# A four-stage transformer block on one core: group statistics, masks and the first output chunk placed elsewhere in the retention stage

## The reference

```
qkv = (x @ wqkv.T).reshape(b, s, N_HEADS, 3 * HEAD_DIM).transpose(0, 2, 1, 3)
q, k, v = jnp.split(qkv, 3, axis=-1)
q, k = _xpos_rotary(q, k, s)
scores = jnp.einsum('bhid,bhjd->bhij', q, k) * decay        # decay is 0 above the diagonal
ret = jnp.einsum('bhij,bhjd->bhid', scores, v)
mean = ret.mean(axis=(2, 3), keepdims=True)                 # one mean and variance for each head
var = ret.var(axis=(2, 3), keepdims=True)
ret = (ret - mean) / jnp.sqrt(var + EPS)
ret = ret * gn_weight[None, :, None, None] + gn_bias[None, :, None, None]
y = ret.transpose(0, 2, 1, 3).reshape(b, s, HIDDEN)
g = x @ wg.T
mish = g * jnp.tanh(jax.nn.softplus(g))
return mish * y @ wo.T
```

## Time and profile before

| | |
|---|---|
| median of 3 runs | 1471.06 us (1469.83 to 1471.92) |
| profiled execution | 1483.77 us |
| its span, first to last instruction | 1482.0 us |
| mean granted TensorE clock | 0.877 |
| busy: PE, DVE, ACT, POOL | 1206.4 (81%), 817.6 (55%), 520.3 (35%), 551.0 (37%) us |
| retention in the trace | about 648 to 838 us |
| scans: first, second | 696 to 744 us, 763 to 794 us |

### The profile page before, as it was taken

How to read it: one execution, slowest core, us unless ns; L and a number is a source line. 1 busy time by engine, 2 the same in 40 slices (tenths; PEclk the granted TensorE clock), 3 DMA queues, 4 the chain that set the end, 5 groups by cost and what they waited for, 6 DMA issues and landing times. The chain is left out here.

```text
span 1482.0 us, 19589 instructions
## 1 busy us (share of the span) xinstructions
PE 1206.4 (81%) x6248; PEld 702.8 (47%) x6287; DVE 817.6 (55%) x1572; ACT 520.3 (35%) x1052; POOL 551.0 (37%) x564
## 2 busy tenths in 40 slices
PE   5589999999999599989998515699999998879541
PEld 2242222222222356755565511188889887754220
DVE  6499999999995564433344379712222211115554
ACT  1137777777778231202342100023333332220000
POOL 6003357655356300021200105444444443224665
PEclk9799999999999799999986755589999999888755
DMA  4950531344000400000000100189999999952333
GB/s 133 182 142 12 87 52 28 39 55 53 12 12 12 164 0 1 1 1 1 0 1 1 59 0 1 50 252 307 309 314 315 297 293 230 231 170 64 85 114 99
DMA packets 142583, 154.78 MB, mean 104 GB/s; under 512 B 50673, under 2 KB 111442, under 8 KB 142418
## 3 DMA queue, kind: packets, MB, share of 16 engines
q1 hardware_dynamic: 106882, 98.71, 26.5%
q0 software_dynamic: 12288, 33.57, 9.0%
q10 hardware_dynamic: 23312, 21.24, 4.4%
HBM read 118.34 MB, written 32.51 MB: 102 GB/s over the span
## 5 line engine op out<-in xcount | busy, mean ns | idle before, releaser
L495 ACT ACTIVATE l_ret_store<-attn_st 128x512 f32<-128x512 f32 x512 | 280.0, 599 | 104.1 <-PE attn_st L406 87.8
L519 DVE TENSOR_REDUCE attn_neg<-attn_mx 128x8 f32<-128x1024 f32 x256 | 299.1, 1201 | 13.5 <-PE attn_mx L386 12.6
L1705 DVE COPY exp_y_sb<-exp_y_ps 128x256 f32<-128x256 f32 x160 | 68.0, 425 | 293.0 <-PE exp_y_ps L1650 277.5
L1616 POOL DMA_INDIRECT exp_rows<-x_rows,moe_tok_i x160 | 151.4, 946 | 193.5 <-PE exp_xt_ps L1630 173.9
L1641 PE MATMUL exp_h_ps<-exp_xt,exp_w 128*88 128x128 f32 x1280 | 174.6, 281 | 20.1 <-DMA exp_w<-in_w 19.2
L1650 PE MATMUL exp_y_ps<-exp_w,exp_ht 96*128 96x256 f32 x640 | 171.1, 391 | 3.0 <-ACT exp_ht L1677 3.0
L386 PE MATMUL attn_mx<-attn_k_st,attn_q_st 96*128 96x512 bf16 x512 | 154.9, 384 | 17.7 <-DVE attn_neg L519 15.0
L406 PE MATMUL attn_st<-attn_q_st,attn_k_st 128*128 128x512 bf16 x473 | 160.1, 383 | 5.8 <-DMA attn_q_st<-attn_neg_rows 2.7
L1641 PEld LDWEIGHTS exp_h_ps<-exp_xt,exp_w 128*88 128x88 f32 x1280 | 150.9, 161 | 29.2 <-DMA exp_w<-in_w 27.1
L418 PE MATMUL attn_o<-l_ret_store,l_ret_tab 128*32 128x512 f32 x1024 | 136.4, 605 | 2.8 <-ACT l_ret_store L495 0.8
L1670 ACT ACTIVATE exp_xt<-exp_xt_ps 128x256 f32<-128x256 f32 x160 | 61.3, 383 | 212.8 <-PE exp_xt_ps L1630 206.7
(11 more groups left out here) (233 smaller groups left out, 1666.4 us busy)
## 6 DMA issues: line engine op xcount, KB each, us to landing
exp_w<-in_w SPq DMA_DIRECT2D x320, 176.0 KB
y_rows<-exp_y_sb ACTq DMA_DIRECT2D x160, 128.0 KB
parts<-l0b_front SPq DMA_DIRECT2D x32, 192.0 KB
attn_k_st<-parts SPq DMA_DIRECT2D x48, 128.0 KB, 7.4
attn_q_st<-parts SPq DMA_DIRECT2D x48, 128.0 KB, 8.0
l_ret_tab<-in_tables SPq DMA_DIRECT2D x4, 1024.0 KB
exp_rows<-x_rows,moe_tok_i POOLq DMA_INDIRECT x160
keep_x_t<-in_x_t SPq DMA_DIRECT2D x4, 512.0 KB
```

The source lines that it names most:

```text
L495: act.activation(probs[s % 2][:, h], st_ps[n % BANKS][:], ACT.Exp, scale=SCALE0).then_inc(exp_done, 1)
L519: dve.tensor_reduce(neg[m % 2][:, i], mx_ps[slot["score", n] % 2][:].rearrange("p (j k) -> p j k", k=P), AX.X, ALU.max, negate=True).then_ ...
L1616: pool.indirect_dma_start(rows[b % RB][:], None, a["x_rows"], bass.IndirectOffsetOnAxis(ap=tok_i[:, b:b + 1], axis=0)).then_inc(rows_in[b ...
L1705: dve.tensor_copy(y_sb[b % YB][:], y_ps[b % 2][:, 0:E]).then_inc(y_in, 1)
```

## The change

Four moves, all in retention; nothing is computed otherwise.

- PE, batch 1: `group(0)` is issued ahead of the four gates of batch 1 instead of behind them.
- DVE, both batches: `mask(first)` comes ahead of the lowering of the gates; the two `lower` follow the first and the second mask.
- PE: `out(0)` to `out(3)` are issued inside the second scan, each behind `retain` of the steps 4 to 7 of it, with the wait for all gates behind the first step.
- DVE: the adds of tiles 0 to 3 go into and right behind the second scan's masks, followed by `norm_measure(0)`, all ahead of `moments(1)`; behind the second coefficients comes `norm_scale(0)` and only then `add(1)`.

```diff
--- before.py
+++ after.py
@@ -1140,10 +1140,11 @@
                     turn_k(t)
                 pe.wait_ge(consts, 6)
                 states(b)
+                if b:
+                    group(b - 1)
                 for n in range(b * QC * KT, (b + 1) * QC * KT):
                     gate(n)
                 if b:
-                    group(b - 1)
                     pe.wait_ge(gvar, b)
                 pe.wait_ge(rot_done, HALF_ROT * (b + 1))
                 scores(first)
@@ -1153,9 +1154,10 @@
                     if b == 0:
                         project(HALF_ROT + t)
                     retain(t)
-            pe.wait_ge(g_done, len(gates))
-            for t in range(TC):
-                out(t)
+                    if b and t == first:
+                        pe.wait_ge(g_done, len(gates))
+                    if b and t - first >= KTS - TC:
+                        out(t - first - (KTS - TC))
             group(BATCH - 1)
             for t in range(TC, 2 * TC):
                 out(t)
@@ -1306,10 +1308,13 @@
                 at = ret[:, m, c * CH:(c + 1) * CH]
                 dve.tensor_tensor(at, at, mish[:, m, c * CH:(c + 1) * CH], ALU.mult).then_inc(weighed, 1)
 
+            def add_tile(t):
+                dve.wait_ge(made, t + 1)
+                norm_add(dve, norm, t, a_ps[t % 2][:, 0:E])
+
             def add(c):
                 for t in range(c * TC, (c + 1) * TC):
-                    dve.wait_ge(made, t + 1)
-                    norm_add(dve, norm, t, a_ps[t % 2][:, 0:E])
+                    add_tile(t)
 
             dve.wait_ge(loaded, 16 * (len(RET_W) + 6))
             for n in range(HALF_ROT):
@@ -1319,22 +1324,25 @@
                 sum_states(b)
                 if b:
                     coefficients(b - 1)
-                for c in range(b * QC, (b + 1) * QC):
-                    lower(c)
                 for t in range(b * KTS, (b + 1) * KTS):
                     mask(t)
+                    if t % KTS < QC:
+                        lower(b * QC + t % KTS)
                     if b == 0:
                         rotate(HALF_ROT + t)
                     elif t % 2:
                         weigh(t % KTS // 2)
+                    if b and t % KTS > KTS - TC:
+                        add_tile(t % KTS - (KTS - TC) - 1)
+                if b:
+                    add_tile(TC - 1)
+                    norm_measure(dve, norm, 0)
                 moments(b)
                 for c in range(b * QC, (b + 1) * QC):
                     close_mish(c)
-            add(0)
             coefficients(BATCH - 1)
-            norm_measure(dve, norm, 0)
+            norm_scale(dve, norm, 0)
             add(1)
-            norm_scale(dve, norm, 0)
             for n in range(QC * KT, 2 * QC * KT):
                 weigh(n)
             norm_measure(dve, norm, 1)
```

## The result

The changed kernel takes 1455.92 us, median of 6 runs (1452.86 to 1460.18), against 1470.73 us for the kernel before in 6 runs of the same comparison (1465.13 to 1476.65). The ratio is 0.9898 with a 95% interval of 0.9879 to 0.9917: some 15 us less (12 to 18). The profiled execution took 1456.11 us, its span 1454.4 us, its mean granted clock 0.890 (0.877 before). All ratios in this text are of executions in the fast state; two slow ones, 2411.94 us among the four of e4 and 1498.36 us among the eight of e6, are left out of them.

The account below looks back on a forecast made before the run. PE was taken to bound the second scan, at half clock. Scan end 782.7 plus 20.0 behind it minus 0.7 gives 802.0 against 815.06, 13.1 us less, so 1458.0 us; the forecast's own range was 1454.5 to 1461.

Parts of the forecast that it names:

- First scan, 0.7 us: First scan of retention: the first mask, now ahead of the lowerings, starts 0.7 us earlier, and all of it is kept.
- Entry: Entry of second scan: scores at 762.0 instead of 762.71, mask 762.8 instead of 765.16, PE's holes 0.8 and 0.15 us.
- Does the clock hold?: Entry of second scan: the granted clock was taken to hold at full level; the lower bound was "falls as before".
- The scan: Second scan at full clock: from 765.05, seven retains 10.4 us and six scores 4.3; end 782.7 with the outputs.
- Outputs inside: Second scan: three output blocks before the last retain, 0.98 us each, put 2.95 us onto PE's path.
- Behind the scan: From the scan's end to the last weighing: 20.0 us, 1.0 less than before, with add(1) taken at 4.8.
- Chunks 1 to 3: Work after the last weighing: order unchanged, clock dips may move, one pair of outs 1.8 us either way.
- rival 1: The clock falls at the second scan's entry and the outs raise it: 3.6 us less, 1467.5 us, chance 0.12.
- Rivals 2 and 3: Clock falls and stays low: in the scan, 1472.7 us, chance 0.07; also through the tail, 1474.8 us, chance 0.06.
- Rival 4: Runs without profile keep full clock in the old second scan: 1 us less, 1470 us, chance 0.10.

Follow-up runs that it names:

- e4: The changed kernel with the first output chunk back behind the second scan (group and mask edits kept); ratio to the kernel before 0.9869.
- e6: The kernel before with the group edit alone (group matmul ahead of the gates); ratio to the kernel before 0.9924.
- e11: e6 plus one full-array matmul of unused result on PE between the first two scores of the second scan; ratio to the kernel before 0.9898.
- e2: The changed kernel with the group matmul back behind the gates (mask and output edits kept); ratio to the kernel before 0.9919.
- e3: The changed kernel with both lowerings back ahead of the masks (group and output edits kept); ratio to the kernel before 0.9878.
- e7: The kernel before with the mask edit alone (first masks ahead of the lowerings); ratio to the kernel before 0.9889.
- e10: e6 unchanged, profiled once more on another chip; one execution, 1462.42 us.
- e8: The changed kernel with POOL's root of the first norm ahead of the second power of the group coefficients; ratio to the kernel before 0.9894.
- e9: The changed kernel with its end reordered: moments(1) directly behind the scan, adds spread, out(4) and out(5) ahead of the second group matmul, root first; ratio to before 0.9853.
- e12: The changed kernel with two added DVE instructions (0.95 us each) ahead of the first mask of the second scan; ratio to the kernel before 0.9869.
- e5: The kernel before with the output edit alone (first output chunk inside the second scan, its adds and norm_measure(0)); ratio to the kernel before 0.9976.
- e1: The kernel before with three extra full-array matmuls of unused result on PE between the first two scores of the second scan; ratio to before 0.9922.

## Why the prediction was right

The forecast was 1458.0 us, 13.1 less than before; measured were 1455.92 and 14.8 less (12 to 18), in the forecast's own range. For the profiled execution it had 1470.7 us, and that one took 1456.11: 12 us of the 27.7 less lie in the last two stages, which no edit touches. The mechanism was the predicted one, a shorter hole that keeps the clock; that it did keep it was in part luck, as said below. By its steps, each against the trace, in us from the first projection where a place is meant:

- *First scan, 0.7 us.* The projections right behind its last retain start 0.95 us earlier (743.35 - 648.53 against 743.81 - 648.04). Right, a little small.
- *Entry.* Second scores predicted at 763.55 - 0.7 = 762.85 on the time axis of the profile before, 3.05 us earlier; 3.44 were measured, 0.25 of the difference from the first scan. PE's two holes were predicted at 0.8 and 0.15 us and measured 0.79 and 0.30. The group matmul delays the gates by 0.24 us (754.15 to 754.39) where 0.28 was taken, DVE's coefficients end at 760.5 beside PE's gates. ACT's scalings and the weighings hold nothing up.
- *Does the clock hold?* It did, and it was worth by far the most: 11.0 us, by e11 against e6. But the reason given was weak: a likeness to a window of whole-array matmuls, which the prediction itself says these are not. Of the five profiles with holes of 1.27 to 1.37 us (e2, e3, e7, e6, e10) two lost the clock; the five with 0.79 us (after, e4, e8, e9, e12) all kept it. With half a microsecond more of hole the 11 us would have been in doubt, and nothing in the trace of before told on which side 0.79 lies. That is the lucky part.
- *The scan.* 0.71 and 1.48 us a step: 2.22 measured, 2.19 taken. The last retain was predicted at 782.0 (with the first scan's share), which is 133.96; measured 133.58.
- *Outputs inside.* 2.95 us onto PE's path; e4 against after says 2.63.
- *Behind the scan.* 20.0 us predicted, 18.1 measured. The term that was mis-sized is add(1): 4.8 us taken for a low clock, 3.5 measured (794.33 to 797.80), since the clock had come back near 793, behind the pair out(4, 5), and fell again only in the middle of out(6, 7). The coefficients (2.11) and the wait for the root of the norm (0.45 predicted, 0.43 measured) were as worked out. The remaining 0.6 is overlap: retain, out(3) and its add overlap by 0.2, and the DVE rows, laid end to end in the sum, by some 0.08 each.
- *Chunks 1 to 3.* Taken as unchanged with one output pair either way; they took 22.4 us instead of 23.8 (from the last weighing to the routing DMA).
- *Two slips that changed nothing.* The group matmul was to come "some 8 us" behind the last retain; the prediction's own terms give 6.4, and 6.25 were measured. The upper end of the forecast's own range, 1461, does not follow from "one out pair either way", which gives 1459.8.

The rivals: rival 1 (the outputs raise a fallen clock) has the mechanism of e5. It took the clock to be back only after the second output block; in e5 it rose right behind the first, 0.7 us into the next scores, so rival 1 was priced some 2 us too slow (it took 5.74 us for a step and an output block that run in about 3.2 at the high clock). Rivals 2 and 3 were not met: in e5, the one kernel where the clock fell and output blocks followed in the scan, it rose. Rival 4 (the hole is the profile's) is refuted by the timed runs: e1 changes nothing but the hole, and the ratio of its runs is 0.9922 (0.9891 to 0.9954). The 12.7 us between the profiled execution of before and its median lie elsewhere. The last stage of that profile, 162.1 us, is like those on the slowest of the three chips, but the record does not name its chip, so this stays a guess.

The Trainium skill, "TensorE: Matmul & The Clock Gate", section "What's actually happening", says that activity releases the throttle. The traces agree behind output blocks (e5, and the end of the scan in the earlier trace rows). They do not agree within the scan, whose matmuls kept PE busy 5.00 us of 5 at a clock of 0.50.

## What to carry to other kernels

When a busy engine's steps take 1.7 times as long as the same steps elsewhere, read the granted clock of the stretch and look at the hole in front of it; shortening or filling that hole can be worth several times the hole itself (here a hole of 2.5 us, 11 us of scan). A filler costs next to nothing where PE waits anyway (0.17 us at the second scores in e1), and tells at once whether the clock is the cause. Moving work from behind a PE-bound loop into it gave nothing here (e4 against the changed kernel): what it saved behind, it cost inside. And when totals of a long program are compared, take both kernels on one chip and look for the difference in the stage that was edited.

## What the runs showed of the hardware

Equal holes did not have equal results. With 1.37 us ahead of the second scores and 0.72 us of scores before them, e6 and e10 fell to 1.2 GHz and e3 stayed at 2.4 GHz, in the same code up to that point of the scan. What decides it is open, and whether one program does both from execution to execution is not shown. Once down, the clock did not come back in 25 to 28 us of scan with PE at 5.00 of 5 (before, e6, e10), while in e5 it rose within 0.7 us of the end of the first output block. The scan's matmuls use 64 rows or 64 columns, but its state products (128*128, 128x128) use the whole array too, and the output blocks also have longer rows (128x256). So the runs do not tell which property of the output blocks raises the clock. Once up, the clock stayed at 1.00 through some 16 us of the same scan matmuls, with no output block among them (e4, e7, e11).
